# Key chunks of 512, 512 and 476 columns in place of three of 500 in a gated cross-attention kernel

## The chip, the cores and the metric

The kernel runs on one core of one Trainium2 chip. The metric is the device time of one execution in microseconds (us). PE is the matrix engine, PEld its weight loads, DVE the vector engine, ACT the scalar engine, POOL the GpSimd engine, SP the engine that issues most of the DMAs.

## The reference

Eight batches of 56 queries attend to 1500 context rows each; 32 query heads share 8 key/value heads of width 128. After it comes a small gated expert layer. What the change touches is the middle:

```python
q = (layernorm(x) @ wq)          # (8, 56, 32 heads, 128)
k = (ctx @ wk)                   # (8, 1500, 8 heads, 128)
v = (ctx @ wv)                   # (8, 1500, 8 heads, 128)
q, k = apply_rope(q), apply_rope(k)
raw = einsum('bhqd,bhkd->bhqk', q, k) / sqrt(128)
attn = softmax(raw + mask)       # over the 1500 keys
x = x + tanh(g_xattn) * (attn @ v @ wo)
x = x + tanh(g_ffn) * experts(layernorm(x))
```

All is float32. The kernel gets its precision by splitting each operand in a rounded high part and a low rest, and by three matmuls for each product: high by high, low by high, high by low (`PASSES`).

## The kernel before

The program has three parts: the queries of all batches, then attention, then the output projection with the expert layer. The attention part takes most of the time and is where the change lies.

**Steps.** Attention is one long row of 64 steps, batch `b` 0 to 7 and key/value head `g` 0 to 7 in each, behind one opening stretch called `first`. What an engine does in a step is written out by hand as a row of words in a table per engine (`PE_STEP`, `ACT_STEP`, `DVE_STEP`); there are rows for steps of even `g`, of odd `g`, for `turn` (head 7 of batches 0 to 6, in which also the next batch's context is turned) and for `last` (head 7 of batch 7). No scheduler moves anything: each engine works through its own row, and semaphores join them.

**Words on PE.** `Sn` is one score chunk: half of the head group (`n // 3`) by key chunk (`n % 3`), 3 matmuls (line 825). `Kcd` is quarter `d` of key chunk `c` for the next head, 3 matmuls (line 785); four quarters make a chunk. `Vmt` is half `t` of value pair `m`, 12 matmuls of 256 columns (line 801). `Cm` transposes tile `m` of the next batch's context (125 rows, 4 matmuls, line 812). `Tj` transposes the probabilities (4 matmuls, line 837), `PVj` weighs the values (line 854).

**What follows each word.** After a `C`, ACT copies the high part (line 705, `cT_hi`) and DVE makes the low rest (line 931, `cT_lo`); that frees one of two banks (`t_free`) and allows the tile to be read. After the four quarters of a key chunk, ACT swaps halves (`swap`, line 696, two operations), DVE multiplies by the cosine and sine tables and adds (`cos`, `sin`, `rot`, lines 916, 920, 926), ACT takes the high part (`K`, line 701), and POOL the low one (line 655, `k_lo`); a score waits for it. After `V`, ACT copies (line 715, `v_hi`), and DVE takes the rest (line 940, `v_lo`), which frees one of the two banks that values and scores share (`sv_free`). After a score, DVE adds the mask and takes the maximum (line 978, `mask`), which frees the same banks; `exp` on ACT (line 740) waits for the maxima.

**Chunks and tiles.** The 1500 keys are 12 tiles of 125 rows and 3 chunks of 500 columns, so a chunk is four tiles. In `first` and `turn` a key part must wait until the tiles of its chunk are there: `(c + 1) * CT - 1` is the last, so tiles 3, 7 and 11. Of the 12 tiles 9 have a place to land early; 9, 10 and 11 are loaded by SP once tiles 0, 1 and 2 have been transposed.

The orders of ACT and DVE that the steps below refer to:

```python
ACT "turn":  "... C4 C5 exp0 C6 C7 exp1 C8 C9 swap0 C10 C11 T0 swap1 ..."
DVE "turn":  "... C2 C3 mask2 mask3 max0 C4 C5 mask4 mask5 max1 norm C6 C7 C8 C9 cos0 C10 C11 ..."
ACT "first": "... C5 C6 swap0 C7 V1 C8 C9 K0 C10 C11 swap1 Q K1 swap2 V2 K2 V3"
DVE "first": "... C5 C6 cos0 sin0 C7 V1 rot0 C8 C9 C10 C11 cos1 sin1 rot1 Q cos2 sin2 V2 rot2 V3"
```

Of the kernel before, what the change touches and what calls it, by code (L numbers as in the profile page):

```python
# [24 lines left out]
GW = REP * DH  # L25
ST = 125
NT = SK // ST
SC = 500
NC = SK // SC
CT = SC // ST  # L30
PAIR = 2 * DH
VT = NT // 2
PT = NT // 2
# [481 lines left out]
def attention_part(nc, ctx, shared, cT, ctx_in, mask, wo, q_dram, inv_dram, attn_dram):  # L515
# [134 lines left out]
    @block.gpsimd  # L650
    def _(pool):
        def k_low(item, s, c):

            pool.wait_ge(k_hi, item + 1)
            nc.gpsimd.tensor_tensor(k[1][:, c * SC:(c + 1) * SC], k_rot[:, s], f32(k[0][:, c * SC:(c + 1) * SC]),  # L655
                                    ALU.subtract).then_inc(k_lo, 1)

        for c in range(NC):
            k_low(k_item(0, 0, c), c % 2, c)

        def wo_low_head(h):
# [19 lines left out]
        batch(B - 1, True)  # L681

        pool.wait_ge(shared.attn_hi, 1)
        for h in range(REP):
            attn_low_head(h)

    @block.scalar
    def _(act):
        def k_exchange(item, s):

            act.wait_ge(k_ready, item + 1)
            if not isinstance(item, int) or item >= 2:

                act.wait_ge(k_rotated, item - 1)
            for lo in range(2):
                nc.scalar.activation(k_swap[lo * HALF:(lo + 1) * HALF, s],  # L696
                                     k_banks[(1 - lo) * HALF:(2 - lo) * HALF, s, 0:SC], ACT.Copy).then_inc(k_swapped, 1)

        def k_high(item, s, c):
            act.wait_ge(k_rotated, item + 1)  # L700
            nc.scalar.activation(k[0][:, c * SC:(c + 1) * SC], k_rot[:, s], ACT.Copy).then_inc(k_hi, 1)  # L701

        def c_high(item, s, m):
            act.wait_ge(t_ready, item + 1)
# [13 lines left out]
        for what, (n, *_) in tasks(ACT_STEP["first"]):  # L718
            if what == "Q":
                q_high(0, 0)  # L720
            if what == "C":
                c_high(n, n % 2, n)
            if what == "swap":
                k_exchange(n, n % 2)
            if what == "K":
                k_high(n, n % 2, n)
            if what == "V":
                v_high(n, n)

        def step(b, g, last):  # L730
            kn = k_item(b, g + 1)
            kind = step_kind(g, last)
            for what, (n, *_) in tasks(ACT_STEP[act_kind(g, last)]):
                s = ((g + 1) * NC + n) % 2
                if what in ("C", "T"):
                    t_bank = t_place(kind, what, n) % 2
                if what == "exp":

                    act.wait_ge(max_ready, b * (HKV * HALVES) + (g * HALVES + n + 1))
                    nc.scalar.activation(prob[n][:, :], prob[n][:, :], ACT.Exp, bias=neg_max[:, n:n + 1],  # L740
                                         accum_out=row_sum[:, n:n + 1]).then_inc(p_ready, 1)
                if what == "Q":
                    q_high(b, g + 1)
                if what == "swap":
                    k_exchange(kn + n, s)
                if what == "K":
                    k_high(kn + n, s, n)
                if what == "out":
                    act.wait_ge(o_ready, b * HKV + (g + 1))
                    nc.scalar.activation(o_lo[:, :], o_banks[:, g % 2, GQ:2 * GQ], ACT.Copy).then_inc(o_lo_copied, 1)  # L750
                if what == "wo":
                    if n == 2:

# [22 lines left out]
    def _(pe):  # L776
        def k_part(item, s, g, c, d, context_item):
# [4 lines left out]

                    pe.wait_ge(t_free, context_item + (RING + 1))
            for n, (a, m) in enumerate(PASSES):
                mm = nc.tensor.matmul(k_banks[:, s, 0:SC], w[0][a][:, d, g * DH:(g + 1) * DH],  # L785
                                      cT[m][:, d, c * SC:(c + 1) * SC], start=(d == 0 and n == 0),
                                      stop=(d == DC - 1 and n == len(PASSES) - 1))
            if d == DC - 1:
                mm.then_inc(k_ready, 1)
# [26 lines left out]
        def scores(b, g, i):  # L816
# [5 lines left out]
            if h == 0:  # L822
                pe.wait_ge(k_lo, k_item(b, g, c) + 1)
            for n, (a, m) in enumerate(PASSES):
                mm = nc.tensor.matmul(sv_banks[0:ROWS, i % 2, 0:SC], q[a][:, h * ROWS:(h + 1) * ROWS],  # L825
                                      k[m][:, c * SC:(c + 1) * SC], start=(n == 0), stop=(n == len(PASSES) - 1))
            mm.then_inc(sv_ready, 1)

        def transposes(b, g, s, j, last):
# [30 lines left out]
        for what, n in tasks(PE_STEP["first"]):  # L860
            if what == "C":
                c_transposes(0, n[0], n[0] % 2, *n)
            if what == "K":
                k_part(n[0], n[0] % 2, 0, *n, (n[0] + 1) * CT - 1)
            if what == "V":
                v_part(n[0], 0, *n, 2 * n[0] + n[1])

        def step(b, g, last):
            kind = step_kind(g, last)
            turn = kind == "turn"  # L870
            for what, n in tasks(PE_STEP[kind]):
# [3 lines left out]
                    scores(b, g, *n)  # L875
                if what == "K":
                    k_part(k_item(b, g + 1, n[0]), ((g + 1) * NC + n[0]) % 2, (g + 1) % HKV, *n,
                           c_item(b, (n[0] + 1) * CT - 1) if turn else None)
                if what == "V":
                    v_part(sv_item(b, g, SCORES + v_fill(g, n[0])), (g + g % 2) % HKV, *n,  # L880
                           c_item(b, 2 * n[0] + n[1]) if turn else None)
# [20 lines left out]
    def _(dve):  # L902
# [7 lines left out]
        def k_cos_part(item, s, c):  # L910

            dve.wait_ge(k_swapped, item * 2 + 2)
            if not isinstance(item, int) or item >= 2:

                dve.wait_ge(k_lo, item - 1)
            nc.vector.tensor_tensor(k_rot[:, s], k_banks[:, s, 0:SC], tables[:, 0, c * SC:(c + 1) * SC],
                                    ALU.mult).then_inc(k_free, 1)

        def k_sin_part(s, c):
            nc.vector.tensor_tensor(k_swap[:, s], k_swap[:, s], tables[:, 1, c * SC:(c + 1) * SC],  # L920
                                    ALU.mult).then_inc(k_sined, 1)
# [22 lines left out]
        for what, (n, *_) in tasks(DVE_STEP["first"]):  # L944
# [6 lines left out]
            if what == "sin":  # L951
                k_sin_part(n % 2, n)
            if what == "rot":
                k_rotate(n, n % 2)
            if what == "V":
                v_low(n, n)

# [7 lines left out]
        def step(b, g, last):  # L965
# [4 lines left out]
            for what, (n, *_) in tasks(DVE_STEP[kind]):  # L970
# [3 lines left out]
                if what == "mask":  # L974
                    h, c = divmod(n, NC)

                    wait_apart(dve, sv_ready, sv_item(b, g, n) + 1, dve_passed)
                    nc.vector.tensor_tensor_reduce(prob[h][:, c * SC:(c + 1) * SC], sv_banks[0:ROWS, n % 2, 0:SC],  # L978
                                                   mask_t[:, c * SC:(c + 1) * SC], 1.0, LOWEST, ALU.add, ALU.max,
                                                   chunk_max[:, h, c:c + 1]).then_inc(sv_free, 1)  # L980
                if what == "max":
                    dve.wait_ge(sv_free, sv_item(b, g, (n + 1) * NC) + RING)
# [411 lines left out]
```

## Time and profile before

| | us |
|---|---|
| median of 3 runs | 2012.15 |
| lowest and highest | 2011.61, 2013.6 |
| the profiled execution, time | 2011.46 |
| its span (first to last instruction) | 2009.7 |
| PE busy | 1977.0 (98%) |
| DVE busy | 1235.7 (61%) |
| ACT busy | 1034.5 (51%) |
| POOL busy | 311.6 (16%) |

The span lies 1.8 us under the execution's own time. A matmul's end is modelled, so consecutive matmuls overlap in the rows; how fast PE goes is read from the distance between starts, and a wait shorter than the overlap isn't marked as idle but still moves the next start. In a timeline row the columns are start, duration, engine, line, operation, written tile <- read tiles, shapes, count, and in brackets the idle time before it with what ended it. Several alike in a row are merged, with their count.

### The profile page before, as it was taken

How to read it: one execution, taken by the hardware profiler on the slowest of the kernel's cores; microseconds unless marked ns; L12 is line 12 of the kernel's file. 1: busy time of each engine (PE TensorE's matmuls, PEld its weight loads, DVE VectorE, ACT ScalarE, POOL GpSimd, SP SyncE). 2: the span in 40 equal slices, each digit the busy share in tenths (PEclk: the TensorE clock that was granted, in tenths of full speed). 3: DMA queues.
4: the chain of work that ended last, by engine and by line, in shares of the span. 5: the costliest groups of instructions: out<-in, count | busy, mean ns of one | idle time of the engine just before them, and what ended most of it. 6: DMA issues, size and time to landing. Idle time of an engine off the chain costs nothing. (4 is left out here: it accounts for less than half of the span.)

```text
span 2009.7 us, 33001 instructions
## 1 busy us (share of the span) xinstructions
PE 1977.0 (98%) x12404; PEld 1777.0 (88%) x12404; DVE 1235.7 (61%) x2639; ACT 1034.5 (51%) x1754; POOL 311.6 (16%) x227
## 2 busy tenths in 40 slices
PE   7999999999999999999999999999999999999898
PEld 7888889888899899988899988998899998998786
DVE  6755566666666556666666666666666656665544
ACT  6555545545555555554545555555644555455532
POOL 5511111111111111111111111110111111111200
PEclk9999999999999999999999999999999999999998
DMA  7711112211112212111211212221111112211180
GB/s 232 256 41 36 33 20 44 32 25 29 30 21 35 33 19 44 35 28 23 43 10 33 35 17 44 35 35 20 39 20 24 34 20 41 36 33 15 48 263 19
DMA packets 74903, 94.39 MB, mean 47 GB/s; under 512 B 22692, under 2 KB 49444, under 8 KB 74760
## 3 DMA queue, kind: packets, MB, share of 16 engines
q1 hardware_dynamic: 73608, 85.10, 20.4%
q10 hardware_dynamic: 1152, 7.34, 0.9%
q8 instruction: 96, 1.57, 0.4%
q14 instruction: 47, 0.39, 0.1%
HBM read 76.64 MB, written 15.77 MB: 46 GB/s over the span
## 5 line engine op out<-in xcount | busy, mean ns | idle before, releaser
L655 POOL TENSOR_TENSOR k_lo<-k_work,k_hi 128x500 fp32r<-128x500 f32 x192 | 244.1, 1285 | 1546.8 <-ACT k_hi L701 1546.8
L801 PE MATMUL low_banks<-wv_hi,cT_hi 128*125 128x256 f32 x1536 | 443.9, 289 | 0.0
L801 PE MATMUL low_banks<-wv_hi,cT_lo 128*125 128x256 f32 x1536 | 431.7, 281 | 0.0
L801 PE MATMUL low_banks<-wv_lo,cT_hi 128*125 128x256 f32 x1536 | 431.5, 281 | 0.0
L1003 DVE TENSOR_TENSOR pT<-t_banks,pT 125x448 fp32r<-125x448 f32 x384 | 236.2, 622 | 243.7 <-ACT pT L765 243.7
L978 DVE CUSTOM_DVE_ANT_0 prob<-low_banks,mask_t 112x500 f32<-112x500 f32 x384 | 259.1, 678 | 177.4 <-PE low_banks L825 176.0
L765 ACT ACTIVATE pT<-t_banks 125x448 fp32r<-125x448 f32 x384 | 205.0, 543 | 309.2 <-PE t_banks L837 308.2
L740 ACT ACTIVATE prob<-prob,neg_max 112x1500 f32<-112x1500 f32 x128 | 198.6, 1552 | 288.7 <-DVE neg_max L983 287.9
L785 PE MATMUL low_banks<-cT_hi,wk_hi 128*128 128x500 f32 x768 | 312.0, 406 | 0.0
L785 PE MATMUL low_banks<-cT_hi,wk_lo 128*128 128x500 f32 x768 | 298.6, 389 | 0.0
L785 PE MATMUL low_banks<-cT_lo,wk_hi 128*128 128x500 f32 x768 | 298.3, 388 | 0.0
L801 PEld LDWEIGHTS low_banks<-wv_hi,cT_hi 128*125 128x125 f32 x1536 | 285.8, 186 | 4.3
L801 PEld LDWEIGHTS low_banks<-wv_hi,cT_lo 128*125 128x125 f32 x1536 | 286.5, 187 | 2.7
L801 PEld LDWEIGHTS low_banks<-wv_lo,cT_hi 128*125 128x125 f32 x1536 | 285.9, 186 | 0.0
L854 PE MATMUL o_banks<-pT,v_hi 125*128 125x448 f32 x768 | 272.4, 387 | 1.8 <-DVE pT L1003 0.7
L696 ACT ACTIVATE k_work<-low_banks 64x500 f32<-64x500 f32 x384 | 223.7, 583 | 13.8 <-PE low_banks L785 5.1
L837 PE MATMUL t_banks<-ident,prob 112*125 112x112 f32 x1536 | 220.5, 270 | 0.9 <-DVE pT L1003 0.9
L837 PEld LDWEIGHTS t_banks<-ident,prob 112*125 112x125 f32 x1536 | 207.0, 188 | 14.2 <-DVE pT L1003 1.0
L940 DVE TENSOR_TENSOR v_lo<-low_banks,v_hi 125x512 fp32r<-125x512 f32 x192 | 132.3, 689 | 136.5 <-ACT v_hi L715 136.5
L715 ACT ACTIVATE v_hi<-low_banks 125x512 fp32r<-125x512 f32 x192 | 114.3, 595 | 192.1 <-PE low_banks L801 191.9
L854 PE MATMUL o_banks<-pT,v_lo 125*128 125x224 f32 x768 | 193.5, 265 | 0.0
L785 PEld LDWEIGHTS low_banks<-cT_lo,wk_hi 128*128 128x128 f32 x768 | 144.5, 188 | 29.9
(136 smaller groups left out, 2908.9 us busy)
## 6 DMA issues: line engine op xcount, KB each, us to landing
stage<-in_ctx_dram SPq DMA_DIRECT2D x72, 250.0 KB
attn_by_head<-attn SPq DMA_DIRECT2D x65, 112.0 KB, 1.7
wq_raw<-in_L_xattn_wq_dram SPq DMA_DIRECT2D x7, 1024.0 KB, 6.0
q_raw<-q_by_head SPq DMA_DIRECT2D x64, 112.0 KB, 5.0
inv_b<-inv_by_head SPq DMA_DIRECT2D x64, 112.0 KB, 5.1
head_rows<-in_ctx_dram SPq DMA_DIRECT2D x24, 250.0 KB
mask_t<-in_mask_BxSxS_ff_dram SPq DMA_DIRECT2D x16, 328.1 KB
stage<-in_L_xattn_wo_dram SPq DMA_DIRECT2D x4, 1024.0 KB, 6.7
```

What stands on the lines that cost most here:

```text
L655: nc.gpsimd.tensor_tensor(k[1][:, c * SC:(c + 1) * SC], k_rot[:, s], f32(k[0][:, c * SC:(c + 1) * SC]), ALU.subtract).then_inc(k_lo, 1)
L696: nc.scalar.activation(k_swap[lo * HALF:(lo + 1) * HALF, s], k_banks[(1 - lo) * HALF:(2 - lo) * HALF, s, 0:SC], ACT.Copy).then_inc(k_swapp ...
L715: nc.scalar.activation(v[0][:, 2 * m:2 * m + 2, :], sv_banks[0:ST, m % 2, :].rearrange("p (t n) -> p t n", t=2), ACT.Copy).then_inc(v_hi, 1)
L740: nc.scalar.activation(prob[n][:, :], prob[n][:, :], ACT.Exp, bias=neg_max[:, n:n + 1], accum_out=row_sum[:, n:n + 1]).then_inc(p_ready, 1)
L765: nc.scalar.activation(pT[:, n % PT_SLOTS, :, 0, :], t_banks[0:ST, t_bank, 0:2 * GQ].rearrange("p (t n) -> p t n", t=2), ACT.Copy).then_in ...
L785: mm = nc.tensor.matmul(k_banks[:, s, 0:SC], w[0][a][:, d, g * DH:(g + 1) * DH], cT[m][:, d, c * SC:(c + 1) * SC], start=(d == 0 and n == ...
L801: mm = nc.tensor.matmul(sv_banks[0:ST, m % 2, t * PAIR:(t + 1) * PAIR], cT[a][:, d, tile * ST:(tile + 1) * ST], w[1][mv][:, d, g * DH:g * ...
L837: mm = nc.tensor.transpose(t_banks[0:ST, s, col:col + ROWS], prob[h][:, (2 * j + t) * ST:(2 * j + t + 1) * ST], ident[0:ROWS, 0:ROWS])
L854: mm = nc.tensor.matmul(o_banks[:, g % 2, 0:(2 - a) * GQ], v[a][:, 2 * j + t, (g % 2) * DH:(g % 2 + 1) * DH], probs, start=(first and a == ...
L940: nc.vector.tensor_tensor(v[1][:, 2 * m:2 * m + 2, :], sv_banks[0:ST, m % 2, :].rearrange("p (t n) -> p t n", t=2), f32(v[0][:, 2 * m:2 * ...
L978: nc.vector.tensor_tensor_reduce(prob[h][:, c * SC:(c + 1) * SC], sv_banks[0:ROWS, n % 2, 0:SC], mask_t[:, c * SC:(c + 1) * SC], 1.0, LOWE ...
L1003: nc.vector.tensor_tensor(pT[:, n % PT_SLOTS, :, 1, :], t_banks[0:ST, t_bank, 0:2 * GQ].rearrange("p (t n) -> p t n", t=2), f32(pT[:, n % ...
```

## The change

The chunk width `SC` becomes 512, the number of chunks stays 3, and the last chunk has the remaining 476 columns. `CHUNK`, `WIDTH` and `LAST_TILE` take the place of the fixed arithmetic; in each operation on a key chunk or a score chunk the slice is that of the chunk. The first chunk now ends inside tile 4 (key 511) and the second inside tile 8 (key 1023); `LAST_TILE` is 4, 8, 11. Two rows of PE's table are rewritten, `turn` and `first`; PE's other rows and all of ACT's, DVE's, POOL's and SP's orders stay.

```diff
-SC = 500
-NC = SK // SC
-CT = SC // ST
+SC = 512
+NC = -(-SK // SC)
+CHUNK = [slice(c * SC, min((c + 1) * SC, SK)) for c in range(NC)]
+WIDTH = [cols.stop - cols.start for cols in CHUNK]
+LAST_TILE = [(cols.stop - 1) // ST for cols in CHUNK]
...
-    "turn": ("C0 C1 S0 S1 C2 C3 S2 S3 C4 C5 K00 S4 K01 S5 C6 C7 K02 K03 C8 C9 K10 K11 C10 C11 K12 K13 T0 T1 K20 K21 "
-             "K22 PV0 K23 T2 V00 T3 V01 PV1 T4 PV2 V10 PV3 V11 T5 V20 V21 V30 V31 PV4 PV5"),
+    "turn": ("C0 C1 S0 S1 C2 C3 S2 S3 C4 C5 S4 K00 S5 K01 C6 C7 K02 K03 C8 C9 V00 K10 K11 C10 C11 K12 K13 T0 T1 K20 "
+             "K21 K22 PV0 K23 T2 T3 V01 PV1 T4 PV2 V10 PV3 V11 T5 V20 V21 V30 V31 PV4 PV5"),
     "last": "S0 S1 S2 S3 S4 S5 O0 T0 T1 T2 PV0 T3 PV1 T4 PV2 T5 PV3 PV4 PV5 O1",
-    "first": ("C0 C1 C2 V00 C3 V01 C4 K00 C5 K01 K02 C6 K03 V10 C7 V11 C8 K10 C9 K11 C10 K12 C11 K13 V20 K20 K21 "
-              "K22 K23 V21 V30 V31"),
+    "first": ("C0 C1 C2 V00 C3 V01 C4 V10 C5 V11 K00 K01 C6 K02 C7 K03 C8 V20 C9 K10 K11 C10 K12 C11 K13 V21 K20 K21 "
+              "K22 K23 V30 V31"),
...
-                mm = nc.tensor.matmul(k_banks[:, s, 0:SC], w[0][a][:, d, g * DH:(g + 1) * DH],
-                                      cT[m][:, d, c * SC:(c + 1) * SC], start=(d == 0 and n == 0),
+                mm = nc.tensor.matmul(k_banks[:, s, 0:WIDTH[c]], w[0][a][:, d, g * DH:(g + 1) * DH],
+                                      cT[m][:, d, CHUNK[c]], start=(d == 0 and n == 0),
...
-                mm = nc.tensor.matmul(sv_banks[0:ROWS, i % 2, 0:SC], q[a][:, h * ROWS:(h + 1) * ROWS],
-                                      k[m][:, c * SC:(c + 1) * SC], start=(n == 0), stop=(n == len(PASSES) - 1))
+                mm = nc.tensor.matmul(sv_banks[0:ROWS, i % 2, 0:WIDTH[c]], q[a][:, h * ROWS:(h + 1) * ROWS],
+                                      k[m][:, CHUNK[c]], start=(n == 0), stop=(n == len(PASSES) - 1))
...
-                k_part(n[0], n[0] % 2, 0, *n, (n[0] + 1) * CT - 1)
+                k_part(n[0], n[0] % 2, 0, *n, LAST_TILE[n[0]])
...
-                           c_item(b, (n[0] + 1) * CT - 1) if turn else None)
+                           c_item(b, LAST_TILE[n[0]]) if turn else None)
...
-            nc.vector.tensor_tensor(k_rot[:, s], k_banks[:, s, 0:SC], tables[:, 0, c * SC:(c + 1) * SC],
+            nc.vector.tensor_tensor(k_rot[:, s, 0:WIDTH[c]], k_banks[:, s, 0:WIDTH[c]], tables[:, 0, CHUNK[c]],
```

The same replacement stands in the other operations on key and score chunks (`k_low`, `k_exchange`, `k_high`, the sine part, `rot` and the mask). The lines of the changed file lie two further down from the tables on.

**PE in the turn of batch 0, from the transposes of tiles 4 and 5 on** (`t_banks<-ident,stage` is a `C`, `cT` by `wk` a key part, `k` by `q` a score). Before:

```order
L812 MATMUL t_banks<-ident,stage 128x125 x8
L785 MATMUL low_banks<-cT_hi,wk_hi 128x500
L785 MATMUL low_banks<-cT_hi,wk_lo 128x500
L785 MATMUL low_banks<-cT_lo,wk_hi 128x500
L825 MATMUL low_banks<-k_hi,q_hi 112x500
L825 MATMUL low_banks<-k_hi,q_lo 112x500
L825 MATMUL low_banks<-k_lo,q_hi 112x500
```

and now:

```order
L814 MATMUL t_banks<-ident,stage 128x125 x8
L827 MATMUL low_banks<-k_hi,q_hi 112x512
L827 MATMUL low_banks<-k_hi,q_lo 112x512
L827 MATMUL low_banks<-k_lo,q_hi 112x512
L787 MATMUL low_banks<-cT_hi,wk_hi 128x512
L787 MATMUL low_banks<-cT_hi,wk_lo 128x512
L787 MATMUL low_banks<-cT_lo,wk_hi 128x512
```

Score 4 has moved ahead of the first key part `K00`; after both, `S5` and `K01` follow in the same way.

**PE in the same turn, from tiles 8 and 9 on.** Before:

```order
L812 MATMUL t_banks<-ident,head_rows 128x125 x4
L812 MATMUL t_banks<-ident,stage 128x125 x4
L785 MATMUL low_banks<-cT_hi,wk_hi 128x500
L785 MATMUL low_banks<-cT_hi,wk_lo 128x500
L785 MATMUL low_banks<-cT_lo,wk_hi 128x500
```

and now:

```order
L814 MATMUL t_banks<-ident,head_rows 128x125 x4
L814 MATMUL t_banks<-ident,stage 128x125 x4
L803 MATMUL low_banks<-wv_hi,cT_hi 125x256
L803 MATMUL low_banks<-wv_hi,cT_lo 125x256
L803 MATMUL low_banks<-wv_lo,cT_hi 125x256
L803 MATMUL low_banks<-wv_hi,cT_hi 125x256
L803 MATMUL low_banks<-wv_hi,cT_lo 125x256
L803 MATMUL low_banks<-wv_lo,cT_hi 125x256
```

The 12 matmuls of `V00` now stand between the transposes and `K10`. They came from behind `T2`, where `T3` now follows at once.

**PE in `first`, from tile 8 on.** Before:

```order
L812 MATMUL t_banks<-ident,head_rows 128x125 x4
L785 MATMUL low_banks<-cT_hi,wk_hi 128x500
L785 MATMUL low_banks<-cT_hi,wk_lo 128x500
L785 MATMUL low_banks<-cT_lo,wk_hi 128x500
L812 MATMUL t_banks<-ident,stage 128x125 x4
```

and now, from tile 7 on:

```order
L814 MATMUL t_banks<-ident,head_rows 128x125 x4
L787 MATMUL low_banks<-cT_hi,wk_hi 128x512
L787 MATMUL low_banks<-cT_hi,wk_lo 128x512
L787 MATMUL low_banks<-cT_lo,wk_hi 128x512
L814 MATMUL t_banks<-ident,head_rows 128x125 x4
L803 MATMUL low_banks<-wv_hi,cT_hi 125x256
L803 MATMUL low_banks<-wv_hi,cT_lo 125x256
```

`K03`, the last quarter of key chunk 0, now comes after `C7`, and before `C8`; `V10` and `V11`, which stood after it, stand ahead of `K00`.

**DVE in `first`**, of the change, at the work that `C9` and `K10` wait for (`cT_lo<-t_banks` is a `C`, `k_work<-low_banks` the `cos` part, then `sin`, `C7`, `V1`, `rot0` and the tiles 8 to 11):

```order
L918 TENSOR_TENSOR k_work<-low_banks,k_tables 128x512
L922 TENSOR_TENSOR k_work<-k_work,k_tables 128x512
L933 TENSOR_TENSOR cT_lo<-t_banks,cT_hi 128x4x125
L942 TENSOR_TENSOR v_lo<-low_banks,v_hi 125x512
L928 TENSOR_TENSOR k_work<-k_work 128x512
L933 TENSOR_TENSOR cT_lo<-t_banks,cT_hi 128x4x125 x4
```

Nothing moved here; only the widths were 500.

## Rows read from the trace of the kernel before

**Rows 1.** The page's busy times: engine, us, share of the span, instructions.

```profile
PE 1977.0 (98%) x12404; PEld 1777.0 (88%) x12404; DVE 1235.7 (61%) x2639; ACT 1034.5 (51%) x1754; POOL 311.6 (16%) x227
```

**Rows 2.** Waits between 130 and 1880 us: all of PE's.

```profile
PE t_banks L812 <- DMA stage<-in_ctx_dram: 0.9, 2, 0.5
```

**Rows 3.** Groups of PE by form: xcount | busy us, mean ns of one | idle.

```profile
L785 PE MATMUL low_banks<-cT_lo,wk_hi 128*128 128x500 f32 x768 | 298.3, 388 | 0.0
...
L1058 PE MATMUL low_banks<-cT_lo,wk_hi 128*128 128x448 f32 x112 | 41.0, 366 | 0.0
...
L1066 PE MATMUL yT_banks<-wk_hi,cT_lo 128*112 128x512 f32 x16 | 6.3, 392 | 0.0
```

**Rows 4.** Timeline of the turn of batch 1, PE.

```profile
545.99 1.02 PE L812 MATMUL t_banks<-ident,stage 125*128 125x125 f32 x8
546.76 0.47 PE L785 MATMUL low_banks<-cT_hi,wk_hi 128*128 128x500 f32 x1
...
551.79 0.65 PE L812 MATMUL t_banks<-ident,head_rows 125*128 125x125 f32 x4
552.37 0.65 PE L812 MATMUL t_banks<-ident,stage 125*128 125x125 f32 x4
...
556.46 1.15 PE L837 MATMUL t_banks<-ident,prob 112*125 112x112 f32 x8
557.38 0.47 PE L785 MATMUL low_banks<-cT_hi,wk_hi 128*128 128x500 f32 x1
```

**Rows 5.** The same turn: DVE, and ACT's `exp1`.

```profile
546.15 0.67 DVE L978 CUSTOM_DVE_ANT_0 prob<-low_banks,mask_t 112x500 f32<-112x500 f32 x1
...
547.41 1.26 DVE L931 TENSOR_TENSOR cT_lo<-t_banks,cT_hi 128x500 fp32r<-128x500 f32 x2
...
551.14 1.54 ACT L740 ACTIVATE prob<-prob,neg_max 112x1500 f32<-112x1500 f32 x1
...
553.29 1.26 DVE L931 TENSOR_TENSOR cT_lo<-t_banks,cT_hi 128x500 fp32r<-128x500 f32 x2 [0.98 <-ACT cT_hi L705]
```

**Rows 6.** Timeline of `first`, PE.

```profile
105.42 0.59 PE L812 MATMUL t_banks<-ident,stage 125*128 125x125 f32 x4
105.77 0.47 PE L785 MATMUL low_banks<-cT_hi,wk_hi 128*128 128x500 f32 x1
...
106.53 0.59 PE L812 MATMUL t_banks<-ident,stage 125*128 125x125 f32 x4
...
109.43 0.28 PE L801 MATMUL low_banks<-wv_hi,cT_hi 128*125 128x256 f32 x1
...
111.20 0.36 PE L801 MATMUL low_banks<-wv_hi,cT_hi 128*125 128x256 f32 x1
...
112.70 0.59 PE L812 MATMUL t_banks<-ident,head_rows 125*128 125x125 f32 x4
```

**Rows 7.** `first`, ACT: the two operations of `swap0`.

```profile
109.63 1.19 ACT L696 ACTIVATE k_work<-low_banks 64x500 f32<-64x500 f32 x2
```

**Rows 8.** `first`, DVE: the low part of tile 7.

```profile
112.10 0.68 DVE L931 TENSOR_TENSOR cT_lo<-t_banks,cT_hi 128x500 fp32r<-128x500 f32 x1
```

**Rows 9.** PE from `K23` of `first` to `S1` of the next step.

```profile
122.81 0.39 PE L785 MATMUL low_banks<-cT_hi,wk_hi 128*128 128x500 f32 x1
...
123.49 0.28 PE L801 MATMUL low_banks<-wv_hi,cT_hi 128*125 128x256 f32 x1
...
129.34 0.48 PE L825 MATMUL low_banks<-k_hi,q_hi 128*112 128x500 f32 x1
```

**Rows 10.** The same stretch, ACT's `K2` and DVE's `V3`.

```profile
127.40 0.62 ACT L701 ACTIVATE k_hi<-k_work 128x500 fp32r<-128x500 f32 x1 [1.68 <-DVE k_work L926]
...
128.59 0.69 DVE L940 TENSOR_TENSOR v_lo<-low_banks,v_hi 125x512 fp32r<-125x512 f32 x1 [1.23 <-ACT v_hi L715]
```

**Rows 11.** Two windows: PE, PEld, DVE, ACT, POOL busy (count), granted clock, DMA share, GB/s.

```profile
97.00:104.00 7.00, 6.21 (x30) 5.83 (x31) 2.52 (x5) 1.77 (x3) 0.00 (x0) 0.53 0.53 199
...
1890.00:1897.00 7.00, 4.70 (x17) 2.67 (x18) 4.06 (x14) 1.91 (x3) 6.27 (x6) 1.00 0.68 199
```

More of the change, by code:

```diff
@@ L654, in k_low @@
             pool.wait_ge(k_hi, item + 1)
-            nc.gpsimd.tensor_tensor(k[1][:, c * SC:(c + 1) * SC], k_rot[:, s], f32(k[0][:, c * SC:(c + 1) * SC]),
+            nc.gpsimd.tensor_tensor(k[1][:, CHUNK[c]], k_rot[:, s, 0:WIDTH[c]], f32(k[0][:, CHUNK[c]]),
                                     ALU.subtract).then_inc(k_lo, 1)
@@ L688, in _, with k_exchange @@
     def _(act):
-        def k_exchange(item, s):
+        def k_exchange(item, s, c):
             act.wait_ge(k_ready, item + 1)
@@ L695, in k_exchange @@
             for lo in range(2):
-                nc.scalar.activation(k_swap[lo * HALF:(lo + 1) * HALF, s],
-                                     k_banks[(1 - lo) * HALF:(2 - lo) * HALF, s, 0:SC], ACT.Copy).then_inc(k_swapped, 1)
+                nc.scalar.activation(k_swap[lo * HALF:(lo + 1) * HALF, s, 0:WIDTH[c]],
+                                     k_banks[(1 - lo) * HALF:(2 - lo) * HALF, s, 0:WIDTH[c]], ACT.Copy).then_inc(k_swapped, 1)
         def k_high(item, s, c):
             act.wait_ge(k_rotated, item + 1)
-            nc.scalar.activation(k[0][:, c * SC:(c + 1) * SC], k_rot[:, s], ACT.Copy).then_inc(k_hi, 1)
+            nc.scalar.activation(k[0][:, CHUNK[c]], k_rot[:, s, 0:WIDTH[c]], ACT.Copy).then_inc(k_hi, 1)
         def c_high(item, s, m):
@@ L723, in _ @@
             if what == "swap":
-                k_exchange(n, n % 2)
+                k_exchange(n, n % 2, n)
             if what == "K":
@@ L744, in step @@
                 if what == "swap":
-                    k_exchange(kn + n, s)
+                    k_exchange(kn + n, s, n)
                 if what == "K":
@@ L915, in k_cos_part, with k_rotate @@
                 dve.wait_ge(k_lo, item - 1)
-            nc.vector.tensor_tensor(k_rot[:, s], k_banks[:, s, 0:SC], tables[:, 0, c * SC:(c + 1) * SC],
+            nc.vector.tensor_tensor(k_rot[:, s, 0:WIDTH[c]], k_banks[:, s, 0:WIDTH[c]], tables[:, 0, CHUNK[c]],
                                     ALU.mult).then_inc(k_free, 1)
         def k_sin_part(s, c):
-            nc.vector.tensor_tensor(k_swap[:, s], k_swap[:, s], tables[:, 1, c * SC:(c + 1) * SC],
+            nc.vector.tensor_tensor(k_swap[:, s, 0:WIDTH[c]], k_swap[:, s, 0:WIDTH[c]], tables[:, 1, CHUNK[c]],
                                     ALU.mult).then_inc(k_sined, 1)
-        def k_rotate(item, s):
+        def k_rotate(item, s, c):
             dve.wait_ge(k_free, item + (RING + 1))
             dve.wait_ge(k_sined, item + 1)
-            nc.vector.tensor_tensor(k_rot[:, s], k_rot[:, s], k_swap[:, s], ALU.add).then_inc(k_rotated, 1)
+            nc.vector.tensor_tensor(k_rot[:, s, 0:WIDTH[c]], k_rot[:, s, 0:WIDTH[c]], k_swap[:, s, 0:WIDTH[c]], ALU.add).then_inc(k_rotated, 1)
         def c_low(item, s, m):
@@ L953, in _ @@
             if what == "rot":
-                k_rotate(n, n % 2)
+                k_rotate(n, n % 2, n)
             if what == "V":
@@ L977, in step @@
                     wait_apart(dve, sv_ready, sv_item(b, g, n) + 1, dve_passed)
-                    nc.vector.tensor_tensor_reduce(prob[h][:, c * SC:(c + 1) * SC], sv_banks[0:ROWS, n % 2, 0:SC],
-                                                   mask_t[:, c * SC:(c + 1) * SC], 1.0, LOWEST, ALU.add, ALU.max,
+                    nc.vector.tensor_tensor_reduce(prob[h][:, CHUNK[c]], sv_banks[0:ROWS, n % 2, 0:WIDTH[c]],
+                                                   mask_t[:, CHUNK[c]], 1.0, LOWEST, ALU.add, ALU.max,
                                                    chunk_max[:, h, c:c + 1]).then_inc(sv_free, 1)
@@ L995, in step @@
                 if what == "rot":
-                    k_rotate(kn + n, s)
+                    k_rotate(kn + n, s, n)
                 if what == "V":
```

## The prediction

> **What bounds the kernel now.** I read the page's busy times first: PE 1977 us of a span of 2009.7, DVE 61%, ACT 51%, POOL 16% [rows 1]. Then the waits of PE over the long middle, 130 to 1880 us: one row, 0.9 us in two waits, both for the DMA of a context tile [rows 2]. So for 1750 us PE goes from one matmul to the next, and the time is the sum of the distances between matmul starts. Waits in `first`, before 130 us, and in the last step come on top. The reader should see two consequences. First, DVE, ACT and POOL have slack in the even and odd steps: what gets faster there is worth nothing. Second, the change can act in two ways only: what a column costs on PE, and what PE has to wait for in the two rewritten rows, `first` (once) and `turn` (seven times).
>
> **Part 1, the widths on PE.** Count first: a triple of chunks was 3 x 500 columns and is 512 + 512 + 476, again 1500; no matmul is added. There are 3 x 768 matmuls of key parts and 3 x 384 of scores, 3456, so 1152 triples, each before and after. If a matmul costs a fixed part and a part by column, the change is exactly nothing. Is it so? The mean lengths of the third pass at three widths are 366 ns at 448 columns, 388 at 500, 392 at 512 [rows 3]. The line from 448 to 512 rises by 26 / 64 = 0.41 ns a column and gives 387.1 at 500: the row lies 0.9 above it. On the line 476 columns would cost 377.4. A triple was 3 x 388 = 1164 and would be 392 + 392 + 377.4 = 1161.4, 2.6 ns less; times 1152 that is 3.0 us. But the rows are rounded to 1 ns, and the 512-wide ones are 16 matmuls of another stage. I take 1.5 ns, **-1.7 us**. The ends: if columns were paid in steps of 8, the triple goes from 3 x 504 to 512 + 512 + 480, 8 columns less, at 0.41 ns 3.3 ns, -3.8 us. If instead the slope from 448 to 500, 22 / 52 = 0.42 ns, held for the way down to 476 and 512 cost 6 ns over 500 instead of 4 (the most that rounding and a different operand allow), the triple costs 12 - 10 = 2 ns more, +2.3 us.
>
> The Trainium skill, page "TensorE: Matmul & The Clock Gate", section "Back-to-back issue gap", has the distance of matmuls as N / 2.4 + 2.5 ns, a fixed part and a strictly linear one. By it part 1 is zero and the sum below would be 1.7 us higher. The rows are no clear witness against it.
>
> **Part 2, the turn.** Key chunk 0 now ends in tile 4, and the order puts `S4` between the transposes of tile 5 and `K00`. Take batch 1. `C4`, `C5` run from 545.99 to 546.76 [rows 4].
> - `S4` stood after `K00` and can now start at 546.76. It needs the bank of `S2`, which the mask of `S2` frees: it starts at 546.15 and takes 0.67 [rows 5], with its short second piece to 546.84, so `S4` waits about 0.14.
> - `S4` ends at 547.66. `K00` needs the low part of tile 4: DVE starts the pair of tiles 4 and 5 at 547.41, 0.67 for the first [rows 5]; with 0.06 for the signal that is 548.14. `K00` waits 0.48. Before, it needed tile 3 only.
> - Together 0.62 late. Of that comes back: between the starts of `C8` and `C9` lie 0.58, where a free-running pair has 0.77 / 2 and its first 0.43 [rows 4], so `C9` waited 0.15 for DVE, and this wait is swallowed. The pair `T0`, `T1` takes 0.92 to the next key part against 0.77 for `C4`, `C5` [rows 4]; I count 0.1 to 0.15 of it as wait that goes. About 0.3 in all.
> - `K10` now needs tile 8, transposed two words earlier. What hides it is `V00`, moved in between. In the old timeline `exp1` starts at 551.14, 0.80 after PE's `C7` ended, and the low part of tile 8 starts 2.15 later, at 553.29 [rows 5]. With PE 0.62 late up to there, exp1 starts at 551.77, the low part at 553.92 and ends at 554.6. PE reaches `K10` at 552.78 (its old end of `C9`, half a us later now) + 0.45 + 1.50 for `V00` = 554.7. So `K10` is just in time, with 0.1 us to spare: I count nothing, and keep up to 0.5 a turn for the range.
> - Moving `V00` out from behind `T2` costs and gains the same: one switch from transposes to wide matmuls less there, one pair of transposes without cover more. `T3` needs the bank of `T1`, whose low part I place 0.4 ahead of it. Zero.
> - The two DMA waits, 0.9 us [rows 2], are at tile 10 or 11 in two of the seven turns; with 1.9 us more between the loads' release and their use they vanish.
>
> The turn: 7 x (0.62 - 0.3) - 0.9 = **+1.3 us**. The score of a turn, its mask and exp come no later than the PE work by which they are delayed; SP's queue (mask load, tile loads) waits for the same words as before.
>
> **Part 3, the opening stretch.** Here `V10` and `V11` go ahead of `K00`, so `K03` ends late, and DVE has `C7` behind `cos0` and `sin0`, which wait for `K03`. The unit costs are: a transposed tile 0.35, a key part behind one 0.76, a value half behind one 1.50 [rows 6], a key part elsewhere 0.68 [rows 9], so a value half elsewhere 1.42. From `C4` at 105.42: `C4` 0.35, `V10` 1.50, `C5` 0.35, `V11` 1.50, `K00`, `K01` 1.38, `C6` 0.35, `K02` 0.78, `C7` 0.35, `K03` 0.78 (12 columns wider: +0.016 each) = 7.34, so `K03` ends at 112.76 instead of 109.43.
> - `C9` needs the low part of tile 7. Before, this came from the end of `K03` at 109.43 by `swap0` from 109.63 [rows 7], `cos0`, `sin0`, to 112.10 + 0.68 [rows 8], 3.35 in all. Now: 112.76 + 3.35 = 116.1, signal 0.06. PE gets there at 112.76 + 0.35 (`C8`) + 1.50 (`V20`) = 114.6: a wait of **1.6 us**.
> - `K10` needs tile 8 instead of 7, and DVE has `V1`, `rot0`, `C8` behind `C7`: three operations at 0.63, as in a pair of 1.26 [rows 5], so 118.0. PE is at 116.2 + 0.38: a wait of **1.4 us**.
> - From 118.04: `K10`, `K11` 1.47, `C10` 0.38, `K12` 0.78, `C11` 0.38, `K13` 0.78, `V21` 1.42, `K20` to `K23` (narrow) 2.66: `K23` ends at 125.9, before at 123.49 [rows 9].
> - The next step's `S1` needs the bank of `V3`. ACT takes `K2` before `V3`, and `K2` waited 1.68 for `rot2` [rows 10], the chain that begins at the end of `K23`. From there to `S1` it was 129.34 - 123.49 = 5.85 [rows 9], with DVE's `V3` the last link [rows 10]. It stays 5.85: `S1` starts at 131.75. **+2.4 us**, and nothing later gives it back, because PE has no waits to swallow it in.
>
> **The rest** is zero with one answer: ACT, DVE and POOL do the same number of operations on the same 1500 columns, and their orders stay. In the last step, where `S1` waits for POOL and `O0` for the last mask, chunks 0 and 1 are 2% slower and chunk 2 5% faster: under 0.1 us.
>
> **Sum** against the profiled execution: -1.7 + 1.3 + 2.4 = +2.0, 2011.46 to 2013.5; against the median 2012.15 it is 2014.1. The profiled execution lies 0.7 below the median, within the spread of the three.
>
> **The rivals.**
> - *A wide matmul is the cheaper one.* If PE paid columns in steps of 16 or more, 500 cost as much as 512 already, and only the 476-wide ones gain: 32 columns of a triple, 13 ns, 15 us, 1999. Against it: 388 and 392 differ by just what 12 columns should cost less 1 ns [rows 3]. Steps of 8 give -3.8 + 3.7 = 2012, no change. 0.10 for a gain of over 4 us, from here and from waits that I have overcounted.
> - *The turn runs late throughout* (slower). `K10` behind `exp1`: if the 0.1 us to spare isn't there, each turn pays up to 0.5 more, 3.5 us, and with widths at zero the sum is 2.4 + 1.3 + 3.5 = +7.2, 2019. The point from which it decides: an extra 0.3 us per turn. For it, that my hand timeline has errors of this size; against it, that PE is only delayed where DVE and ACT have caught up. With widths at +2.3 instead, +6.0. Together 0.16.
> - *The clock falls in `first`* (slower). After PE's idle stretch before 97 us the granted clock was 0.53 over 7 us [rows 11], 1.2 GHz for most of it, so about 3.3 us were lost. PE now stands still 1.6 and 1.4 us, and 1.6 at `S1`. Then it is 2014.1 + 3.3 = 2017.4. Against it: from 1890 to 1897 PE was busy 4.70 of 7.00 us, with the clock at 1.00 [rows 11]. 0.10. The Trainium skill says on the same page, in "HAM oscillation — how this bites in real kernels", that waits between groups of matmuls send the clock down; the second of these windows doesn't show it.
> - *The change doesn't cost what I say in `first`*: the DVE chain is shorter, or the last wait is swallowed. Then -1.7 + 1.3 = 2011.8; 0.07, no change.
>
> **How the numbers follow.** A measurement of this kernel tells apart about 0.2%, 4.0 us: under 2008.1 is faster, over 2016.2 slower. The forecast itself has 0.57 and lies inside; with the last rival and the steps of 8 that makes 0.64 for the same. Slower gets the second and third rival, 0.26; faster 0.10. The range reaches from -2 (widths at -3.8, the turn at nothing) to +6 (widths at +2.3 or a fallen clock): 2010.0 to 2018.0.
>
> **What would show it.** Key and score matmuls, mean of a triple's distances, within 3 ns of before: else part 1 is wrong. In the turn `K00` starts 0.4 to 0.6 after `S4` ends, and `K10` right after `V00`; turns 0.2 to 0.4 us longer, except the two with DMA waits, which get shorter. In `first` a wait of about 1.6 us before `C9`, of 1.4 before `K10`, and `S1` of the next step at about 131.7. Even and odd steps within 0.02 us of before: if they moved by 0.1 each, the forecast is off by 5 us, and wrong.

## The result and the profile after

| | before | changed |
|---|---|---|
| median, us (8 runs each) | 2013.76 | 2018.9 |
| lowest and highest | 2011.61, 2015.02 | 2017.74, 2021.19 |
| the profiled execution's span | 2009.7 | 2018.4 |

The ratio is 1.0028, with a 95% interval of 1.0017 to 1.0039: the changed kernel is 5.1 us slower by the medians. 2014.1 was forecast, 2.0 over the kernel before, with a range to 2018.0. The forecast started from a median of 3 runs, 2012.15; over 8 runs the median of the kernel before is 2013.76, so 1.6 of the 4.8 us between 2014.1 and 2018.9 lie in that starting point, not in the change.

The page of the changed kernel has PE at the same share, with 5.0 us more busy [rows 1]:

```profile
PE 1982.0 (98%) x12404; PEld 1780.7 (88%) x12404; DVE 1233.8 (61%) x2639; ACT 1033.1 (51%) x1754; POOL 311.8 (15%) x227
```

The list of PE's waits (who waited for what: us in all, times, longest) has two rows that weren't there before, the first and the last of these three: key parts wait for the low part of a context tile, a score for the low part of a value. The middle one, of transposes, was 1.4 us in two waits before:

```profile
PE low_banks L787 <- DVE cT_lo L933: 4.1, 8, 1.2
...
PE t_banks L814 <- DVE cT_lo L933: 2.0, 2, 1.4
PE low_banks L827 <- DVE v_lo L942: 1.2, 1, 1.2
```

One of the 8 waits in the first row is in `first`, the seven others are one in each turn. The waits of transposes lie in `first`, before and after.

To place the loss I split the time at matmul starts: `C0` of `first`, `C4` of `first`, `S1` of the step behind it, and the first matmul of each step. `before` is the profile shown above; `again` is a second profile of the same kernel.

| stretch, us | before | again | changed |
|---|---|---|---|
| up to `C4` of `first` | 105.4 | 105.5 | 107.4 |
| `C4` to `S1` of the first step | 23.92 | 23.94 | 27.60 |
| an even step (median of the 31 behind the opening step) | 24.61 | 24.61 | 24.57 |
| an odd step (median of 24) | 30.02 | 30.01 | 30.00 |
| the seven turns together | 250.9 | 250.0 | 254.3 |
| the last step, up to the matmul behind its 0.7 us wait | 37.1 | 37.7 | 38.3 |

The stretch up to `C4` has no key part in it; it differs by how long the clock stays at half speed around 100 us: 6.8 us in both profiles of the kernel before, 10.2 in the changed one. Both lengths occur at 500 columns too (10.2 in the run `best_500`), so I don't count it as the change's. What the change did is +3.7 in the opening, +4.3 in the turns against `again`, and -1.4 in the even steps. Against the first profile, from which the forecast was made, the turns are +3.4.

**The turn.** Timeline of the changed kernel in the turn of batch 1 (PE and DVE), which answers to [rows 4] and [rows 5]:

```profile
551.23 1.02 PE L814 MATMUL t_banks<-ident,stage 125*128 125x125 f32 x8
...
552.14 0.48 PE L827 MATMUL low_banks<-k_hi,q_hi 128*112 128x512 f32 x1
...
552.68 1.25 DVE L933 TENSOR_TENSOR cT_lo<-t_banks,cT_hi 128x500 fp32r<-128x500 f32 x2
...
553.50 0.47 PE L787 MATMUL low_banks<-cT_hi,wk_hi 128*128 128x512 f32 x1 [0.41 <-DVE cT_lo L933]
...
554.27 0.37 PE L827 MATMUL low_banks<-k_hi,q_hi 128*112 128x476 f32 x1
```

`S4` starts 0.91 us after `C4` where a pair takes 0.77: 0.14 late, as forecast. `K00` starts 1.36 after `S4`, and ends its three matmuls in 0.77, although it follows a score and not a transpose.

`K10` is held too, which the list of waits doesn't show, because the wait is shorter than the overlap of the matmuls. The first of these rows is the low part of tiles 8 and 9, of which tile 8 ends at 560.03; the second is `K10`:

```profile
559.36 1.26 DVE L933 TENSOR_TENSOR cT_lo<-t_banks,cT_hi 128x500 fp32r<-128x500 f32 x2 [1.22 <-ACT cT_hi L707]
...
560.18 0.47 PE L787 MATMUL low_banks<-cT_hi,wk_hi 128*128 128x512 f32 x1
```

`K10` starts 0.15 us after the end of tile 8's low part, in all seven turns, and so does `K00` after that of tile 4. `T3` starts 0.06 us after DVE's part of `T1`, which frees its bank, again in all seven (in batch 1 at 568.45 after 568.39).

**The opening.** Timeline of the changed kernel from `C8` to `K11`, which answers to [rows 6 to 8]:

```profile
114.74 0.59 PE L814 MATMUL t_banks<-ident,head_rows 125*128 125x125 f32 x4
114.94 1.21 ACT L698 ACTIVATE k_work<-low_banks 64x512 f32<-64x512 f32 x2 [1.25 <-PE low_banks L787]
...
117.39 0.67 DVE L933 TENSOR_TENSOR cT_lo<-t_banks,cT_hi 128x500 fp32r<-128x500 f32 x1
...
118.12 0.65 PE L814 MATMUL t_banks<-ident,stage 125*128 125x125 f32 x4 [1.37 <-DVE cT_lo L933]
...
119.18 1.26 DVE L933 TENSOR_TENSOR cT_lo<-t_banks,cT_hi 128x500 fp32r<-128x500 f32 x2
...
120.00 0.47 PE L787 MATMUL low_banks<-cT_hi,wk_hi 128*128 128x512 f32 x1 [1.23 <-DVE cT_lo L933]
...
120.92 0.63 PE L787 MATMUL low_banks<-cT_hi,wk_hi 128*128 128x512 f32 x1
121.34 0.63 PE L787 MATMUL low_banks<-cT_hi,wk_lo 128*128 128x512 f32 x1
```

`C9` starts 3.38 us after the end of `K03` (forecast 3.4), `K10` 5.26 after it (forecast 5.28). Then comes what the sum didn't have: from 120.9 on, matmuls of 512 columns start 0.42 us apart, half speed. The window says it with the granted clock (columns as in [rows 11]):

```profile
119.00:126.00 7.00, 6.00 (x26) 5.05 (x27) 2.68 (x5) 2.61 (x5) 1.28 (x1) 0.76 0.01 3
```

In both profiles of the kernel before, the clock is 1.00 in this window. In the changed one it is at its lower level, 1.2 GHz, from 120.6 to 124.0.

### The profile page after: what moved, and what is told of

It is laid out like the page before. It is cut to its first block and busy times, and to the rows that moved or that the text cites. A ratio compares the mean times of both kernels' runs of the same rounds, so it can differ in the third digit from the quotient of the medians.

```text
span 2018.4 us, 33001 instructions
## 1 busy us (share of the span) xinstructions
PE 1982.0 (98%) x12404; PEld 1780.7 (88%) x12404; DVE 1233.8 (61%) x2639; ACT 1033.1 (51%) x1754; POOL 311.8 (15%) x227
## 3 DMA queue, kind: packets, MB, share of 16 engines
q8 instruction: 96, 1.57, 0.4%
## 5 line engine op out<-in xcount | busy, mean ns | idle before, releaser
L657 POOL TENSOR_TENSOR k_lo<-k_work,k_hi 128x512 fp32r<-128x512 f32 (+1 forms) x192 | 244.4, 1287 | 1553.3 <-ACT k_hi L703 1553.3
L980 DVE CUSTOM_DVE_ANT_0 prob<-low_banks,mask_t 112x512 f32<-112x512 f32 (+1 forms) x384 | 256.7, 678 | 182.7 <-PE low_banks L827 179.8
L787 PE MATMUL low_banks<-cT_hi,wk_hi 128*128 128x512 f32 (+1 forms) x768 | 311.9, 406 | 4.1 <-DVE cT_lo L933 4.1
L787 PE MATMUL low_banks<-cT_hi,wk_lo 128*128 128x512 f32 (+1 forms) x768 | 299.2, 390 | 0.0
L787 PE MATMUL low_banks<-cT_lo,wk_hi 128*128 128x512 f32 (+1 forms) x768 | 299.0, 389 | 0.0
L698 ACT ACTIVATE k_work<-low_banks 64x512 f32<-64x512 f32 (+1 forms) x384 | 224.1, 583 | 15.0 <-PE low_banks L787 1.3
L787 PEld LDWEIGHTS low_banks<-cT_hi,wk_hi 128*128 128x128 f32 x768 | 145.2, 189 | 31.1 <-issue 7.2
```

The source lines that it names most:

```text
L657: nc.gpsimd.tensor_tensor(k[1][:, CHUNK[c]], k_rot[:, s, 0:WIDTH[c]], f32(k[0][:, CHUNK[c]]), ALU.subtract).then_inc(k_lo, 1)
L698: nc.scalar.activation(k_swap[lo * HALF:(lo + 1) * HALF, s, 0:WIDTH[c]], k_banks[(1 - lo) * HALF:(2 - lo) * HALF, s, 0:WIDTH[c]], ACT.Copy ...
L787: mm = nc.tensor.matmul(k_banks[:, s, 0:WIDTH[c]], w[0][a][:, d, g * DH:(g + 1) * DH], cT[m][:, d, CHUNK[c]], start=(d == 0 and n == 0), s ...
L980: nc.vector.tensor_tensor_reduce(prob[h][:, CHUNK[c]], sv_banks[0:ROWS, n % 2, 0:WIDTH[c]], mask_t[:, CHUNK[c]], 1.0, LOWEST, ALU.add, ALU ...
```

## The experiments

All times are compared with the kernel before on the same chip.

**The widths alone: 476, 512, 512 columns.** With the narrow chunk first, the chunks end in tiles 3, 7 and 11 as before, and the old orders fit. The lines shown are against the changed kernel; both rows of `PE_STEP` are the old ones as well.

```diff
-CHUNK = [slice(c * SC, min((c + 1) * SC, SK)) for c in range(NC)]
+ENDS = (476, 988, 1500)
+CHUNK = [slice(lo, hi) for lo, hi in zip((0,) + ENDS, ENDS)]
```

> Chunks of 476, 512, 512 (ends 476, 988, 1500) with the orders of the kernel before. The last tiles stay 3, 7 and 11, so no wait on PE changes: this is the widths alone. Theory (widths cost nothing, the loss is waits and clock falls): 1.5 to 2.5 us under the kernel before, even steps 0.03 to 0.05 us shorter, turns and the opening stretch as before. Rival (a matmul of 512 columns costs more than its columns, and that is the loss): 3 to 6 us over the kernel before, spread over all 64 steps.

Measured: 2012.71 against 2011.73, ratio 1.0005 (0.9996 to 1.0014): no difference. The rival is out: 512 columns aren't what costs. The 1.5 to 2.5 us that I expected to gain are out too, in this arrangement. The even steps got 0.04 longer and the odd ones 0.03 shorter; in the changed kernel, with the narrow chunk last, it was the even steps that gained 0.04. The third passes of this run's key parts, in the groups by form (count, busy us, mean ns), against 388 ns at 500 [rows 3]:

```profile
L788 PE MATMUL low_banks<-cT_lo,wk_hi 128*128 128x512 f32 x512 | 202.8, 396 | 0.0
...
L788 PE MATMUL low_banks<-cT_lo,wk_hi 128*128 128x476 f32 x256 | 96.8, 378 | 0.0
```

These lengths hold overlaps and switches, so I go by starts. Where a key part or a score stands between others of them (even and odd steps), a matmul has 216 ns at 476 columns, 227 at 500 and 231.6 to 232 at 512: a line within 1 ns, and 1500 columns cost the same to 1.5 ns a triple. That much is still up to 1.7 us over all triples, so whether the columns' own price gives a little back isn't settled.

**The new orders at 500 columns.** Both new rows of `PE_STEP` in the kernel before.

> Chunks of 500 with the two new rows of PE's order. Key parts wait for tiles 3 and 7 again. Theory (the order costs only together with the later tiles 4 and 8): turns of 35.6 to 35.8 us, K00 right behind S4, S4 late by 0.1; in the opening stretch the wait before C9 (1.6 us) stays, that before K10 is gone; in all 0 to +1 us against the kernel before. Rival (the order itself is the loss): turns of 36.3 us, +5 us in all.

Measured: 2012.25 against 2011.73, ratio 1.0001 (0.9992 to 1.001). The turns took 35.5 us, less than the 35.7 of before and a little less than the 35.6 to 35.8 expected. In the opening the wait before `C9` stayed and that before `K10` went; `C4` to `S1` took 24.6 us, 0.7 more than before, with no fall of the clock. So neither half of the change costs time by itself in the timed runs; it's the later last tile, met by an order that leaves too little between.

**The new turn with the old opening, 512 columns.**

> Chunks of 512, 512, 476 with the new turn and the old opening row. Theory: turns of 36.34 us as in the changed kernel (+3.4 us in all against before), widths -2 us; in the opening stretch K00 now waits 1.9 us for tile 4 and K10 some 2.4 for tile 8, of which 2.1 come back from the waits for loads: +2.2. Sum +3.6 us, up to +5.3 if the clock falls in the opening stretch. Rival (the new opening row is the larger part of the loss): under +2 us.

Measured: 2019.48, ratio 1.0039 (1.0026 to 1.0052), +7.8 us, above the +3.6 to +5.3 expected. The turns were as in the changed kernel, 36.36, which is +4.5 together against the second profile of before, not +3.4. `C4` to `S1` took 27.7 us, 3.8 more than before: the 2.2 expected of the waits and the fall of the clock, which came here as well (0.76 from 116 to 123 us). The widths gave 1.3 us back, not 2. For chunks of 512 the two opening rows are equally bad.

Here the clock fell behind one wait of 2.5 us, before `K10` (the wait before it, of 1.9 us, ended more than seven us earlier), and it did so in the next run too, which has the same opening row.

**Both old rows with 512, 512, 476.**

> Chunks of 512, 512, 476 with both old rows: what the rewritten rows are worth. Theory: each turn waits 1.5 us before K00 (tile 4) and 1.3 before K10 (tile 8), 0.3 come back: turns of 38 us, with the opening stretch of the run before and the widths 14 to 17 us over the kernel before. Rival (the later tiles cost little in any order): under +6 us.

Measured: 2033.02, ratio 1.0105 (1.0087 to 1.0124), +21 us, more than the 14 to 17 expected; turns of 38.35, and `C4` to `S1` 27.6 us. PE's waits have one row for it, two in each turn and two in the opening:

```profile
PE low_banks L787 <- DVE cT_lo L933: 20.6, 16, 2.3
```

So the rewritten turn did save 14 us of what the wide chunks cost (2033.02 against 2019.48 in the run before).

**The turn repaired.** The changed kernel with a second score ahead of `K00`, so that 0.65 us more lie between `C4` and the part that needs it.

```diff
-    "turn": ("... C4 C5 S4 K00 S5 K01 C6 ..."
+    "turn": ("... C4 C5 S4 S5 K00 K01 C6 ..."
```

> The changed kernel with one more move in the turn: S4 S5 K00 K01 in place of S4 K00 S5 K01, so that 0.65 us of a score lie before K00. Theory (the wait for the low part of tile 4 is the turn's loss): the wait of 0.6 us before K00 and the 0.08 of the restart behind it are gone, turns of 35.6 to 35.7 us in place of 36.34, 4.5 to 5 us under the changed kernel. Rival (the wait moves on to K10 or the transposes T, since DVE and ACT are the later ones in the turn): turns of over 36.1.

Measured: 2014.29 against 2012.55, ratio 1.0008 (0.9999 to 1.0017): 1.7 us over the kernel before, where the changed kernel was 5.1 over it. The two were timed at different times, each against its own runs of the kernel before; the traces have the clearer number, turns of 35.69 in place of 36.34, 4.5 us in the seven. The PE rows of its turn of batch 1:

```profile
551.85 0.38 PE L827 MATMUL low_banks<-k_hi,q_hi 128*112 128x476 f32 x1
...
552.49 0.40 PE L787 MATMUL low_banks<-cT_hi,wk_hi 128*128 128x512 f32 x1
...
553.22 0.39 PE L787 MATMUL low_banks<-cT_hi,wk_hi 128*128 128x512 f32 x1
```

`K00` follows `S5` at once, and `K01` comes 0.73 (in the median of the turns 0.70) after it, not 0.77. `K10` still starts 0.15 us after the low part of tile 8 in every turn.

**The opening filled with work.** The changed kernel, with `V20` computed two times more in the waits before `C9` and `K10`; the repeats are overwritten.

```diff
-    "first": ("... C7 K03 C8 V20 C9 K10 K11 ..."
+    "first": ("... C7 K03 C8 V20 V20 C9 V20 K10 K11 ..."
```

> The changed kernel with the 12 matmuls of V20 done two times more, in the waits before C9 and before K10 of the opening stretch: the same result, overwritten, 24 matmuls more and 2.9 us of PE's waits filled. Theory (PE standing still is what makes the clock fall there): no clock fall before 130 us, K11, C10 and K12 at full speed, opening stretch 1.4 to 1.7 us shorter although PE does more. Rival (the fall is a matter of chance or of the stage): it falls there as before, and the stretch is as long or longer.

Measured: 2017.0 against 2012.55, ratio 1.0023 (1.0014 to 1.0033). The timed runs don't tell this from the changed kernel's 1.0028 (1.0017 to 1.0039); the traces do. The same window as above:

```profile
119.00:126.00 7.00, 7.00 (x46) 6.24 (x45) 3.62 (x7) 3.52 (x7) 1.29 (x1) 1.00 0.00 0
```

`K10` starts no earlier (12.66 us after `C4`, in the changed kernel 12.62), but `S1` 1.57 earlier, although PE does 24 matmuls more. That is the price of the fall, with the slower first matmuls behind the waits (some 0.1 us) in it. PE's standing still is what brings it on: in the opening the clock fell in all four profiles whose kernels have the waits before both `C9` and `K10` or the longer one before `K10` (the changed kernel, the new turn with the old opening, both old rows, the repaired turn) and in none of the eight others. So it isn't chance.

**Both repaired.** On top of the repaired turn, an opening that spends the value halves where PE waited:

```diff
-    "first": ("C0 C1 C2 V00 C3 V01 C4 V10 C5 V11 K00 K01 C6 K02 C7 K03 C8 V20 C9 K10 K11 C10 K12 C11 K13 V21 K20 K21 "
-              "K22 K23 V30 V31"),
+    "first": ("C0 C1 C2 V00 C3 V01 C4 V10 K00 C5 K01 K02 C6 K03 V11 C7 V20 C8 V21 C9 K10 K11 C10 K12 C11 K13 K20 "
+              "K21 K22 K23 V30 V31"),
...
-    "first": "... swap2 V2 K2 V3",
+    "first": "... swap2 V2 V3 K2",
```

> The run repaired_turn, and an opening row that keeps the value halves for the places where PE waits (V10 K00 C5 K01 K02 C6 K03 V11 C7 V20 C8 V21 C9 K10, all K2 before V30), with V3 ahead of K2 on ACT. Theory (the opening loses by cos0 and sin0 ahead of C7 and by the clock fall that the waits bring): waits before K00 0.4 and before K20 0.5 us, none before C9 and K10, no clock fall before 130 us; opening stretch and first step together 54 to 55.5 us (before 55.57, changed 59.98), 3 to 5 us under the kernel before. Rival (the chunk of 512 makes the chain to the first scores longer whatever the order): 57 us or more, and no gain on before.

Measured: 2010.39 against 2012.55, ratio 0.9988 (0.9978 to 0.9997): 2.2 us under the kernel before, less than the 3 to 5 expected. `C4` to `S1` took 23.65 us and the clock held; the wait before `K20` was 0.9, not 0.5.

**The new turn at 500 columns, old opening.**

> Chunks of 500, the new turn, the old opening row. Theory (the new turn is good where tiles 3 and 7 are the last, and bad only with 4 and 8): turns of 35.5 us, the two DMA waits gone, opening stretch as before: 2.0 to 2.8 us under the kernel before. Rival (the new turn is no better at any width, and the 35.5 us of the run with both new rows came from its later start): no difference from before.

Measured: 2011.01 against 2012.55, ratio 0.9993 (0.9984 to 1.0002): not told apart from no change by the timed runs. The turns were 248.4 us together, 35.5 each as expected, 1.6 less than the second profile of before. The rival, that they owed this to their later start, is out. My 2.0 to 2.8 counted DMA waits that are not always there.

**The best at 500 columns.** The new turn, and an opening with `V20`, `V21`, `V30` in PE's waits and `V2`, `V3` early on ACT and DVE.

```diff
-    "first": ("... C8 K10 C9 K11 C10 K12 C11 K13 V20 K20 K21 K22 K23 V21 V30 V31"),
+    "first": ("... C8 K10 V20 C9 K11 V21 C10 K12 C11 K13 V30 K20 K21 K22 K23 V31"),
...
-    "first": "... Q K1 swap2 V2 K2 V3",
+    "first": "... Q K1 V2 swap2 V3 K2",
...
-    "first": "... Q cos2 sin2 V2 rot2 V3",
+    "first": "... Q V2 cos2 sin2 V3 rot2",
```

> Chunks of 500 with the new turn and an opening row of my own: V20, V21 and V30 in the places where PE waited for loads and for tile 11 (C8 K10 V20 C9 K11 V21 C10 K12 C11 K13 V30 K20 K21 K22 K23 V31), V2 and V3 early on ACT and DVE. Theory (waits in turn and opening are all there is to win, widths nothing): turns 35.5 us, S1 of the first step about 1.5 us earlier, 3 to 4.5 us under the kernel before, at or under the best so far (2010.39). Rival (the 512-wide chunks are what made that one fast): not under 2011.

Measured: 2010.06 against 2012.57, ratio 0.9988 (0.9979 to 0.9997), as good as the best with 512. `S1` came 1.55 us earlier as expected, but `S2`, which waits for POOL, only 1.0. The gain is that 1.0 and 1.6 in the turns. It fell short of the 3 to 4.5 expected; that 500 columns reach the same time as 512 speaks against the rival.

**The kernel before, profiled again.**

> The kernel before, unchanged, for one more profile. In its first profile the clock did not fall in the last step, in all others so far it did. If that was chance: a fall between 1885 and 1900 us, last step 37.9 to 38.2 us in place of 37.11, and the first profile stands about 1 us too low. If it belongs to the kernel before: 37.1 us again. The two turns with DMA waits are expected again, at 36.1 to 36.3 us.

Its last step took 37.7 us, with the clock at 0.83 from 1887 to 1897: the first of the two outcomes that I had named, chance, though worth 0.6 us and not 1. No turn had a DMA wait (35.7 in all seven), against what I expected. So both peculiarities of the first profile were chance, and both had entered my reading.

## Why the prediction was wrong

**Part 1, widths: -1.7 forecast, -1.4 in the changed kernel, nothing with the narrow chunk first.** In number this part held, by luck as far as is known. The 0.9 ns by which the row at 500 stood above the line [rows 3] can't be told from rounding and another stage. The even steps' -1.4 us in the changed kernel come back as a loss in the run with the narrow chunk first; why the place of the narrow chunk moves an even step by 0.04 us was not settled. The linear formula that the prediction names from the Trainium skill, page "TensorE: Matmul & The Clock Gate", section "Back-to-back issue gap", stands there for isolated matmuls. Its form fits: 216, 227 and 231.6 to 232 ns are a line. Its constants don't: by it 512 columns take 216 ns, and that is what 476 took here.

**Part 2, the turn: +1.3 forecast, +3.4 shown against the same profile, +4.3 against the second.** This is the step that failed. The mechanism was right for `K00`: `S4` late by 0.14, `K00` waiting for tile 4, the waits at `C9` and `T1` swallowed. What the later tiles cost was put too low. With the new turn in both, a turn takes 36.34 us with chunks of 512 and 35.47 at 500: the later tiles cost 0.87, where the forecast had 0.48, the wait of `K00` alone. The new order at 500 gave 0.25 back (35.72 to 35.47), so the net loss of a turn was 0.62 and not 0.3. The terms:
- `K00` was held for 0.6, not 0.48. I had taken 0.06 us from DVE's end to PE's start. That holds for the transpose `C9` in the opening: DVE ended at 118.06, PE started at 118.12. `K00` and `K10` start 0.15 after DVE's end, `K10` of the opening at 120.00 after 119.85.
- A key part behind a wait costs 0.77, as one behind a transpose does, not 0.69. The repaired turn shows wait and restart together: 0.65 us a turn.
- "`K10` is just in time, I count nothing" was wrong: the sum gave it no time at all from DVE's end to PE's start. It was held in every turn, for 0.04, and ran slower behind it, 0.77 for 0.67: 0.14 a turn, about 1 us in all.
- `T3` was put at zero, with the low part of `T1` 0.4 ahead of it. At 500 columns it is 0.2 ahead; at 512 `T3` starts right behind it and takes 0.45 for 0.37. These 0.08 and the 0.14 of `K10` are the 0.22 by which the repaired turn, 35.69, is still longer than the new turn at 500.
- The 0.9 us of DMA waits that I gave back were an accident of one profile; the second profile of the same kernel had none to give.

**Part 3, the opening: +2.4 forecast, +3.7 shown.** The waits were where they were forecast, those before `C9` and `K10` to 0.02 us, and from the end of `K23` to `S1` it was 5.7 us for 5.85. With the same waits filled, so without the fall of the clock, the stretch is 26.03 us, 2.1 over before. The clock was the rival with 0.10, priced at 3.3 us; it came true, at 1.57. The window in the last step with the clock at 1.00 [rows 11], which I had held against it, was the luck of one profile: in every other profile, the second of the same kernel too, the clock fell there.

Put together: 4.3 + 3.7 - 1.4 = 6.6 us from the traces against 5.1 measured, inside the ratio's interval of 3.4 to 7.9. The two larger errors, in the turn and in the opening, were of the same sign, and the range had no room for a turn's loss doubled together with a fallen clock.

**The other rivals.** Steps of 16 columns: out, by 216, 227, 232. "The turn runs late throughout, `K10` behind `exp1`": its point was 0.3 us a turn over the forecast, and it was 0.3. The wait that it names is there: in the turn of batch 1 ACT's `exp1` starts at 557.21, its copy of tile 8 at 558.73, DVE's low part at 559.36, and `K10` waits for that. But it is 0.14 of the 0.3, the rest is `K00` and `T3`. With its chance of 0.16 it was nearer the truth than the forecast.

## What to carry to other kernels

Where one engine has no waits at all, a change that moves when its operands are complete pays for most of each new wait (of 0.87 us a turn the new order's other effects gave 0.25 back); write down, for each moved boundary, what now lies between the last piece's start and its first reader, and compare it with the whole chain (here 2.3 us from `C4`'s start through ACT and DVE to `K00`'s), with the time from the releasing engine's end to the start that it releases, plus the restart behind it. "Just in time" is a wait if that time isn't counted. A single further independent operation in that place was worth 4.5 us in the traces. Take a second profile of the kernel before wherever the sum counts on a wait that shows in a few of many alike steps.

## What the runs showed of the hardware

- In the opening the clock fell where PE had stood still twice in 3.5 us (1.5 and 1.5 us, with four transposes between), and also behind one wait of 2.5 us, with four transposes ahead of it (the new turn with the old opening, both old rows). It held behind one wait of 1.5 us (the new orders at 500), behind waits of 0.4 and 0.9 us (both repaired), and where the same pauses were filled. The half-speed stretch cost 1.57 us. It isn't shown how much standing still is needed.
- A wait costs more than its length, also where the profile marks none: a key part behind it takes some 0.08 to 0.10 us longer, as behind a run of short transposes (0.77 for 0.67 to 0.69). A matmul of a key part that DVE releases started 0.15 us after DVE's end (`K00` and `K10`, each in seven turns), a transpose 0.06.
- The cost of a matmul between 476 and 512 columns is a line within 1 ns: 216, 227 and 231.6 to 232 ns from start to start.
